# Weight stage of a fused cross-attention, self-attention and expert kernel: scales loaded once and spread by selection matmuls, smaller parts, biases as rows

## The reference

```python
x = x + xattn(layernorm(x), ctx, Wq, w_kc_q, w_kc_kv, W_qr, W_kr, Wo)     # 16 heads, 257 context rows
x = x + attn(layernorm(x), ...)                                           # below
x = x + ffn(layernorm(x), router, gate_up, down)                          # top 8 of 64 experts

def _mxfp4_matmul(x, codes, scales, block_size=32):
    w = codes * jnp.repeat(scales, block_size, axis=0)
    return x @ w
q = _mxfp4_matmul(x, wq_codes, wq_scales) + bq      # codes (256, 2048), scales (8, 2048); k and v likewise
...
return _mxfp4_matmul(out, wo_codes, wo_scales) + bo # codes (2048, 256), scales (64, 256)
```

## Time and profile before

| | us |
|---|---|
| median of three runs | 846.65 |
| span of the profiled execution | 876.3 |
| TensorE matmul busy | 664.1 (76%) |
| VectorE busy | 420.8 (48%) |
| ScalarE busy | 305.1 (35%) |
| GpSimd busy | 291.6 (33%) |
| DMA moved | 92.66 MB |

### The profile page before, as it was taken

The page is one execution under the profiler, slowest core; times in us unless marked ns, Lnnn a source line. Parts: engine busy times, 40 slices in busy tenths (PEclk is TensorE's granted clock), DMA queues, the critical chain, the costliest instruction groups (busy, mean ns, idle before and its releaser), DMA issues.

```text
span 876.3 us, 17897 instructions
## 1 busy us (share of the span) xinstructions
PE 664.1 (76%) x6210; PEld 536.8 (61%) x6210; DVE 420.8 (48%) x1090; ACT 305.1 (35%) x811; POOL 291.6 (33%) x279
## 2 busy tenths in 40 slices
PE   7856777889999997997997997998714765556550
PEld 5745557777867875875875875867513654445440
DVE  1414663454765774774774764756441222222232
ACT  1122553235453362362362363350302333333210
POOL 4003584212114224124124122021224455555562
PEclk8855657799999998998998998999966999999985
DMA  8946994791002002002001001000004989998956
GB/s 244 253 84 154 251 221 120 247 344 27 1 2 79 0 8 70 0 15 63 0 15 63 0 22 38 3 30 30 24 26 120 227 190 200 198 196 198 203 95 168
DMA packets 100680, 92.66 MB, mean 106 GB/s; under 512 B 32366, under 2 KB 94576, under 8 KB 100640
## 3 DMA queue, kind: packets, MB, share of 16 engines
q1 hardware_dynamic: 70992, 60.87, 26.8%
q0 software_dynamic: 12288, 17.95, 10.0%
q10 hardware_dynamic: 17360, 13.30, 5.1%
HBM read 60.22 MB, written 32.83 MB: 106 GB/s over the span
## 4 chain that ended last, share of the span: by engine, by line
PE 42%; DMA 21%; DVE 14%; issue 10%; ACT 5%; another core or an unknown queue 3%; ACTq 2%; SPq 1%; POOL 1%; DVEq 0%; POOLq 0%; PEldq 0%
DMA expert_sums<-Wh,etok 18%; PE bank L1135 5%; PE bank L1137 5%; PE bank L1136 5%; PE bank L1169 4%; PE bank L1201 4%; PE bank L1190 3%; PE bank L1154 3%; PE bank L1238 3%; PE bank L1183 2%; PE bank L1112 1%; ACTq L564 1%; PE bank L1124 1%; PE bank L1182 1%
## 5 line engine op out<-in xcount | busy, mean ns | idle before, releaser
L530 POOL DMA_INDIRECT expert_sums<-Wh,etok x64 | 98.8, 1544 | 96.9 <-DVE Wh L1037 83.0
L1338 PE MATMUL bank<-ring,Wh 96*128 96x256 f32 x128 | 45.0, 434 | 66.1 <-DVE Wh L1025 64.5
L606 ACT ACTIVATE pr<-bank,nmax 128x257 f32<-128x257 f32 x128 | 61.2, 478 | 95.9 <-DVE nmax L830 94.7
L1135 PE MATMUL bank<-space,Wh 128*128 128x128 f16 x512 | 89.4, 221 | 4.9 <-DVE X L928 3.2
L473 POOL DMA_INDIRECT expert_rows<-h,slot x64 | 62.7, 980 | 87.2 <-DVE slot L921 66.6
L1137 PE MATMUL bank<-space,Wl 128*128 128x128 f16 x512 | 89.3, 220 | 0.0
L1136 PE MATMUL bank<-space,Wh 128*128 128x128 f16 x512 | 89.3, 220 | 0.0
L1201 PE MATMUL bank<-Cr,pT 128*128 128x64 f32 x512 | 78.9, 281 | 6.2 <-DVE On L840 5.3
L1201 PEld LDWEIGHTS bank<-Cr,pT 128*128 128x128 f32 x512 | 75.0, 211 | 8.2 <-DVE On L840 5.2
L456 POOL TENSOR_TENSOR Cr<-C,Ct 128x192 f32<-128x192 f32 x64 | 38.4, 625 | 115.9 <-PE bank L1201 114.6
L830 DVE TENSOR_REDUCE nmax<-bank 128x1 f32<-128x257 f32 x128 | 53.4, 419 | 48.6 <-PE bank L1183 43.8
(11 more groups left out here) (173 smaller groups left out, 1518.6 us busy)
## 6 DMA issues: line engine op xcount, KB each, us to landing
ring<-L_ffn_gate_up_proj_dram SPq DMA_DIRECT2D x64, 192.0 KB
expert_rows<-h ACTq DMA_DIRECT2D x8, 1284.0 KB, 13.8
Wh<-expert_rows SPq DMA_DIRECT2D x64, 160.5 KB
ring<-L_ffn_down_proj_dram SPq DMA_DIRECT2D x64, 96.0 KB
C<-ctx_dram SPq DMA_DIRECT2D x24, 128.0 KB, 4.0
expert_sums<-h ACTq DMA_DIRECT2D x2, 1152.0 KB, 14.0
space<-L_xattn_Wo_dram SPq DMA_DIRECT2D x8, 256.0 KB, 5.0
space<-L_xattn_Wq_dram SPq DMA_DIRECT2D x4, 512.0 KB, 8.3
```

The source lines that it names most:

```text
L530: e.indirect_dma_start(Y[n % NY][:, :], bass.IndirectOffsetOnAxis(ap=etok[:, n % 4:n % 4 + 1], axis=0), ye[:, n % 4], None, bounds_check=Y ...
L606: e.activation(pr[:, s, :], bank[r % 2][:, 0:NL], ACT.Exp, bias=nmax[:, s:s + 1], accum_out=rsum[:, s:s + 1]).then_inc(expd, 1)
L1135: e.matmul(dst, ah, bh, start=first and n == 0, stop=False)
L1338: e.matmul(bank[4 + n % 2][:, 0:D], hh[:, n % 2], dn[:, n], start=True, stop=True).then_inc(e_dn, 1)
```

## The change

Parts keep 128 x 1024 elements but have no room for scales: a buffer is half as long, and nine buffers in `space` serve parts 7 to 15, once each; parts 0 to 2 have buffers in `ring` and `diag`, used again by parts 3 to 6. All scales are loaded once, by four loads of 64 KB, each to four partitions (32w to 32w+3). A matrix `pick` of zeros and ones, four rows for each weight, is built by VectorE from the identity. For each part TensorE multiplies it with the scale rows, two f32 matmuls of 512 columns, into two PSUM banks (1 and 6 in the fold, 6 and 7 in tile 0), and VectorE multiplies the codes with these. The fold now takes 1, 2, 2 and 2 parts in groups 0 to 3, and tile 0 nine, in rows 0 to 12. The biases bq, bk and bv are loaded as 48 rows of 128 at the very start and transposed by TensorE together with the router weights. The product of bv and Wo moves from between the tiles into steps 0 to 3 of tile 1, in the place of the output projection that tile 1 doesn't have. SP's order of loads changes: the scales and part 0 stand ahead of the context and group 1, parts 1 and 2 ahead of group 2, part 3 (which waits for part 0) ahead of the rest of group 2, parts 4 to 6 among and behind group 3.

```diff
-FOLD_PARTS = (0, 0, 2, 3)
+FOLD_PARTS = (1, 2, 2, 2)
-TILE_PARTS = dict(zip((0, 2, 3, 5, 6, 8, 9, 11, 12, 14, 15), range(PART0[GROUPS], PARTS)))
-NPB = 6
-BUFFER = [u % 3 for u in range(PART0[GROUPS])]
-BUFFER += [(PART0[GROUPS] % 3 + n) % NPB for n in range(PARTS - PART0[GROUPS])]
+TILE_PARTS = dict(zip((0, 2, 3, 5, 6, 8, 9, 11, 12), range(PART0[GROUPS], PARTS)))
+EARLY = 3
+NPB = EARLY + PARTS - PART0[GROUPS]
+BUFFER = [u % EARLY for u in range(PART0[GROUPS])] + list(range(EARLY, NPB))

...
-        parts = [t.rearrange("p (n f) -> p n f", n=2) for t in (
-            ring[:, 0:2048], ring[:, 2048:4096],
-            diag[:, :, :].rearrange("p a b -> p (a b)"), space[:, 0:2048], space[:, 2048:4096], space[:, 4096:6144])]
+        scl = ring[:, 0:4096]
+        flat_diag = diag[:, :, :].rearrange("p a b -> p (a b)")
+        parts = [ring[:, 4096:5120], flat_diag[:, 0:1024], flat_diag[:, 1024:2048]]
+        parts += [space[:, 1024 * n:1024 * n + 1024] for n in range(NPB - EARLY)]

...
-                elif n >= 3:
+                elif n >= EARLY:
                 if w < 3:
-                    e.dma_start(to[:, 0], codes[w][c * P:(c + 1) * P, o:o + 1024]).then_inc(here, 16)
-                    for q in range(4):
-                        e.dma_start(to[32 * q:32 * q + 32, 1],
-                                    scales[w][4 * c + q:4 * c + q + 1, o:o + 1024].to_broadcast([32, 1024])).then_inc(here, 16)
+                    e.dma_start(to, codes[w][c * P:(c + 1) * P, o:o + 1024]).then_inc(here, 16)
                 else:
-                    e.dma_start(to[:, 0].rearrange("p (h d) -> p h d", h=4),
+                    e.dma_start(to.rearrange("p (h d) -> p h d", h=4),
-                    for q in range(4):
-                        e.dma_start(to[32 * q:32 * q + 32, 1].rearrange("p (h d) -> p h d", h=4),
-                                    scales[w].rearrange("(h q) d -> q h d", q=4)[q:q + 1, hs].to_broadcast([32, 4, D])
-                                    ).then_inc(here, 16)
+            def load_scales(w):
+                to = scl[32 * w:32 * w + 4, :]
+                if w < 3:
+                    e.dma_start(to.rearrange("q (c f) -> q c f", c=2), scales[w].rearrange("(c q) f -> q c f", q=4)).then_inc(scales_in, 16)
+                else:
+                    e.dma_start(to.rearrange("q (h d) -> q h d", h=H), scales[w].rearrange("(h q) d -> q h d", q=4)).then_inc(scales_in, 16)
             def load_context(i):

...
             load_fold_first(0)
             load_fold_rest(0)
+            for w in range(4):
+                load_scales(w)
+            load_part(0)
             load_context(0)
             load_fold_first(1)
             load_fold_rest(1)
+            load_part(1)
+            load_part(2)
             load_fold_first(2)
-            load_part(0)
+            load_part(3)
             load_fold_rest(2)
             load_fold_first(3)
-            load_part(1)
+            load_part(4)
             load_fold_rest(3)
-            load_part(2)
-            for u in range(3, 6):
-                load_part(u)
+            load_part(5)
+            load_part(6)
             e.wait_ge(roped, 2 * BT)
             load_context(1)
-            for u in range(6, PARTS):
+            for u in range(PART0[GROUPS], PARTS):
                 load_part(u)

...
         def _(e):
+            for n, bias in enumerate((bq, bk, bv)):
+                e.dma_start(brows[H * n:H * n + H, :], bias.rearrange("(h p) -> h p", p=P)).then_inc(bias_in, 16)
+            e.dma_start(obias[:, :], bo.unsqueeze(0).to_broadcast([P, D])).then_inc(obias_in, 16)
             def part_high(u):
-                e.copy(part_of(Wh, u), parts[BUFFER[u]][:, 0]).then_inc(w_high, 1)
+                e.copy(part_of(Wh, u), parts[BUFFER[u]]).then_inc(w_high, 1)
             for g in range(GROUPS):

...
                 for u in range(PART0[g], PART0[g + 1]):
-                if g == 1:
-                    with nc.allow_non_contiguous_dma(reason="biases of 2048 elements"):
-                        for n, bias in enumerate((bq, bk)):
-                            e.dma_start(bqk[:, n, :], bias.rearrange("(h p) -> p h", p=P)).then_inc(bias_in, 16)
-                        e.dma_start(bvT[:, :], bv.rearrange("(h p) -> p h", p=P)).then_inc(bias_in, 16)
-                    e.dma_start(obias[:, :], bo.unsqueeze(0).to_broadcast([P, D])).then_inc(bias_in, 16)
             def blank(n):

...
         def _(e):
+            e.wait_ge(consts, 1)
+            for w in range(4):
+                q = slice(32 * w, 32 * w + 4)
+                e.tensor_copy(pick[q, :].rearrange("p (q n) -> p q n", q=4),
+                              ident[q, q].unsqueeze(2).to_broadcast([4, 4, 32])).then_inc(pick_ready, 1)
+            e.tensor_copy(bqk[:, :, :], bank[7][:, P:P + 2 * H].rearrange("p (n h) -> p n h", n=2)).then_inc(rwT_ready, 1)
+            e.tensor_copy(bvT[:, :], bank[7][:, P + 2 * H:P + 3 * H]).then_inc(rwT_ready, 1)

...
-            def part_mul(u):
-                e.wait_ge(w_in[BUFFER[u]], 80 * BUFFER[:u + 1].count(BUFFER[u]))
-                e.scalar_tensor_tensor(parts[BUFFER[u]][:, 0], parts[BUFFER[u]][:, 0], WS, parts[BUFFER[u]][:, 1], ALU.mult, ALU.mult).then_inc(w_mul, 1)
+            def part_mul(u, lo, hi):
+                here = parts[BUFFER[u]]
+                e.wait_ge(w_in[BUFFER[u]], 16 * BUFFER[:u + 1].count(BUFFER[u]))
+                e.wait_ge(w_scaled, u + 1)
+                e.scalar_tensor_tensor(here[:, 0:512], here[:, 0:512], WS, lo[:, :], ALU.mult, ALU.mult)
+                e.scalar_tensor_tensor(here[:, 512:1024], here[:, 512:1024], WS, hi[:, :], ALU.mult, ALU.mult).then_inc(w_mul, 1)
             def rope_copies(g):

...
-                if len(left) > 2:
-                    part_mul(left.pop(0))
+                if len(left) > 1:
+                    part_mul(left.pop(0), bank[1], bank[6])
-                if len(left) > 1:
-                    part_mul(left.pop(0))
+                part_mul(left.pop(0), bank[1], bank[6])
-                for u in left:
-                    part_mul(u)
+                assert not left

...
+            def obias_out():
+                bk_, need = spos("wo", -1)
+                e.wait_ge(sf[bk_], need)
+                e.wait_ge(obias_in, 16)
+                e.scalar_tensor_tensor(obias[:, :], SBANK[bk_][:, 0:D], 1.0 / WS, obias[:, :], ALU.mult, ALU.add).then_inc(sd[bk_], 1)
+                e.wait_ge(sd[bk_], need + FREE)
             def self_out_norm(j):

...
-            ins.then_inc(rw_t, 1)
-            e.wait_ge(rwT_ready, 1)
+            e.wait_ge(bias_in, 48)
+            e.transpose(bank[7][:, P:P + 3 * H], brows, ident[0:3 * H, 0:3 * H]).then_inc(rw_t, 1)
+            e.wait_ge(rwT_ready, 3)
+            def spread_scales(u, lo, hi):
+                if u:
+                    e.wait_ge(w_mul, u)
+                else:
+                    e.wait_ge(pick_ready, 4)
+                    e.wait_ge(scales_in, 64)
+                q = slice(32 * (u // 4), 32 * (u // 4) + 4)
+                o = 1024 * (u % 4)
+                e.matmul(lo[:, :], pick[q, :], scl[q, o:o + 512], start=True, stop=True)
+                e.matmul(hi[:, :], pick[q, :], scl[q, o + 512:o + 1024], start=True, stop=True).then_inc(w_scaled, 1)
             def rope_transposes(g):

...
+                    e.wait_ge(w_mul, PART0[g])

...
+                left = list(range(PART0[g], PART0[g + 1]))
+                if len(left) > 1:
+                    spread_scales(left.pop(0), bank[1], bank[6])

...
                 ins.then_inc(f_n, 1)
+                spread_scales(left.pop(0), bank[1], bank[6])
+                assert not left

...
                     ins.then_inc(sf[bk_], 1)
+            def obias_sum(name):
+                bk_, need = spos("wo", -1)
+                dst = SBANK[bk_]
+                if name == "wo0":
+                    e.wait_ge(sd[bk_], need - 1 + FREE)
+                    e.wait_ge(w_done, PARTS)
+                    e.wait_ge(bv_split, 2)
+                a = 4 * int(name[2])
+                ins = split(dst[:, 0:D], [(bvh[:, h:h + 1].to_broadcast([P, P]), bvl[:, h:h + 1].to_broadcast([P, P]),
+                                           Wh[:, 6 + h // 8, (h % 8) * D:(h % 8 + 1) * D],
+                                           Wl[:, 6 + h // 8, (h % 8) * D:(h % 8 + 1) * D]) for h in range(a, a + 4)],
+                            first=a == 0, last=a == 12)
+                if name == "wo3":
+                    ins.then_inc(sf[bk_], 1)
             def skip(name, j):

...
+                        if isinstance(i, int) and i == 0 and r in TILE_PARTS:
+                            spread_scales(TILE_PARTS[r], *SBANK)

...
             tile(0, None, None)
-            e.wait_ge(w_done, PARTS)
-            e.wait_ge(bv_split, 2)
-            ins = split(bank[7][:, 0:D], [(bvh[:, h:h + 1].to_broadcast([P, P]), bvl[:, h:h + 1].to_broadcast([P, P]),
```

(31 more changed lines are left out.)

## The result

The changed kernel took 901.02 us (median of 4 runs, 892.07 to 902.16) beside 846.74 us for the kernel before (median of 4, 844.25 to 850.82): ratio 1.0603, 95% interval 1.0540 to 1.0666. It is slower by 6.0%, and the forecast of 832.0 us with its range of 815 to 855 missed it. What came true is rival R3, selections at low clock, and it cost more than the 884 us given for its worst form.

What follows compares the result with a forecast made beforehand. Before tile 2, it blamed TensorE's idle hole, low clock and tile 0's scale-row waits and TensorE work. Gains of 8.0 (fold), 1.5 (queries), 0.3 (tile 0) and 4.8 (bias product), 14.6 together, gave 832.0 us, range 815 to 855.

Steps and rivals of the forecast that it cites:

- R3: Rival: clock stays at 0.50 although selections run; 858 us, or 884 with the fold at low clock too; chance 0.14.
- (e): Fold: selection matmuls on TensorE's path, 1.8 us a part, the first 3.6 at low clock; seven parts add 14.4 us.
- (b): Fold: without the hole the clock stays up; groups 2 and 3 save 4.3 us each, group 3's transposes about 0.9.
- (g): Fold, group 0: dense L1118 and first selection raise the clock earlier; L1124 and the next transposes save 1.9 us.
- (d): Fold: scale loads and part 0 ahead of group 1's weights add 5.0 us, with a range of 3 to 10.
- (a): Fold, group 1: bias loads leave ScalarE's queue, removing 12.4 us of idle TensorE; their replacement costs nothing.
- (c): End of fold: no part multiply on VectorE between the last M copy and the first normalised tile; 2.6 us saved.
- (f): Fold: VectorE's multiply in two halves, one operand in PSUM, 1.3 us against 1.2, covered by matmuls; costs 0.
- Tile 0 at full clock: Score rows of tile 0: full clock for rows with parts, 3.05 us each; 40.0 us against 36.0, 4.0 lost.
- Tail and bias product: After tile 0's rows: tail gains 4.3 us; bias product leaving the seam between tiles for tile 1 gains 4.8.
- R2: Rival: SP held by part 3's load until part 0 is subtracted, group 3's weights late; 841 us; chance 0.16, shared.
- R1: Rival: cheap selection, 1.0 us a part; 821 us; chance 0.17.

Runs made afterwards that it cites:

- e1_no_select: The changed kernel without its selection matmuls, VectorE multiplying the codes with themselves, scale loads kept: 869.55 us, ratio 1.0021 to the kernel before.
- e3_bias_only: The kernel before with only the biases loaded as rows at the start and transposed with the router weights: 867.95 us, ratio 0.9982.
- e5_scales_later: The changed kernel with scale loads and part 0 moved behind group 1's first loads: 920.78 us, ratio 1.0521 to the kernel before.
- e10_warm: e4b_bias_product plus two useless 128-row bf16 matmuls behind each score row of tile 0: 849.30 us, ratio 1.0025 to the kernel before.
- e4b_bias_product: The kernel before with bias rows and the product of bv and Wo moved into tile 1, timed again in another group: 844.16 us, ratio 0.9967.
- e2_rows128: The changed kernel with selections over 128 stationary rows instead of 4, the added rows zeros: 879.53 us, ratio 1.0153 to the kernel before.
- e4_bias_product: The kernel before with bias rows and the product of bv and Wo moved into tile 1, first timing: 868.30 us, ratio 0.9952.

## Why the prediction was wrong, step by step

The time is 69.0 us off (901.0, 832.0). Up to the first score of tile 1 the sum said 143.3 (157.9 less 14.6), and 204.3 was measured: 61.0 us of it. The other 8 are not placed; the sum stood on a first profile of before whose 157.9 was 5.6 above the second's. By stage: fold to the last M copy 73.4 forecast, 108.7 measured (+35.3); from there to the first score 11.3 and 14.2 (+2.9); rows of tile 0 40.0 and 63.2 (+23.2); row 15 to the first score of tile 1 18.6 and 18.2 (-0.4).

**The step that failed: (e) with its clock.** The sum took "full clock for part rows" because "wide f32 matmuls raised it" and "the selections are of the wide kind". The number of moving columns was the wrong likeness. L1169 fills 128 rows of the array, the selections four. That, and the score rows at 0.50 while fully busy, the same text filed as arguments for R3, with 0.14. Over 128 rows the same instructions run at 0.92. At the low clock the seven parts of the fold took 25.7 instead of 14.4 us. The 1.8 for a part at full clock was right: 1.82 with 128 rows. In tile 0 the price for the low clock was right: 63.4 in R3, 63.2 measured.

**(b) and (g), clock gained back in the fold: not there.** Groups 1 to 3 took 3.67 or 3.68 for each of L1147 and L1161. That is the 4.3 and 4.3 of (b) never gained, 4.2 lost in group 1, which had had full clock before, and 0.9 and 1.9 of the transposes and of (g): 15.6. e1_no_select and e3_bias_only show that the selections are not needed for it: group 1 lost its clock there as well. What lets the clock fall there stays open; it is not the hole alone, since these kernels have none. The Trainium skill (TensorE: Matmul & The Clock Gate, the HAM clock gate) says that a busy stretch frees the clock and an idle one returns it to half. By that rule the filled hole was bound to help; the trace disagrees here, with 15.00 of 15.00 us busy at 0.51 in group 1 and 30.00 of 30.00 at 0.50 in tile 0.

**(d), late loads: a delay was foreseen, its size and its place were not.** 8.3 us later (14.59 to 22.93) against 5.0 taken and 12 as the far end. The sum priced bytes and landings. What the trace shows is SP's queue: the issue of group 1's first two loads, behind the scales, part 0 and the context, lasts 8.52 us, where it took 1.64 before (9.10 to 10.74); the load that TensorE waits for is issued only then and lands 2.4 us later.

```profile
11.90 8.52 SPq L304 DMA_DIRECT2D space<-L_xattn_W_qr_dram  x2
20.47 0.61 SPq L305 DMA_DIRECT2D space<-L_xattn_W_kr_dram  x1
```

Part 0, issued at 7.68 behind the scales, took 13.0 us to land. The long issue goes with the scale loads: put later (e5_scales_later), they leave group 1's issue at 1.64 and make that of group 2's first two loads 5.79, where it took 1.71 before. The Trainium skill (DMA: Bandwidth & Descriptors, on why a DMA increments its semaphore by 16) has such loads on 4 of 16 engines; the estimate worked out from it, 6.2, was nearer to 8.3. No run counted the engines: from 12 to 18 us the rate was low, 80 to 146 GB/s against 271 in the fold before, but the mean busy share of the 16 engines stood at 1.02 to 1.20, which does not show idle ones.

**(a): the hole went, and its price was given back.** 12.4 us of idle time are not in the trace. Not foreseen: the Wo load, and with it the first fold transposes, came at 10.6 instead of 9.1, for which I had allowed 1 us of room; e3_bias_only, which has the new bias rows and no scale loads, shows the same (10.65). It is no loss of its own in the changed kernel, since TensorE then stands for group 1's weights anyway. With 11.3 of (e), 15.6 of the clock and 3.3 of (d), 30.2 of the fold's 35.3 are placed. The other 5.1 are transposes and G matmuls that took longer than before, 5.8 (1.0 in group 1's first transposes, 0.7, 1.7 and 0.8 in the three rounds of fold transposes, 1.3 in group 3's L1135, 0.3 in group 0), less 0.7 by which the wait for VectorE ahead of group 3 (0.85) came out shorter than taken (1.6).

**(c), 2.6 us behind the last M copy: 0.85 measured.** The part multiply is gone from VectorE there, but the two small instructions that split the value bias and the first normalised tile run beside GpSimd's work (2.12 us from 107.60, 0.98 from 109.68, 0.99 from 110.62) and grew:

```profile
108.70 0.69 DVE L804 COPY M<-bank 128x512 f32<-128x512 f32 x1 [2.25 <-PE bank L1161]
109.31 0.45 DVE L1020 CAST bvh<-bvT 128x16 f16<-128x16 f32 x1
109.78 0.91 DVE L1022 TENSOR_TENSOR bvl<-bvT,bvh 128x16 f16<-128x16 f32 x1
110.62 1.15 DVE L958 TENSOR_SCALAR h<-X,mv,rs 128x256 f32<-128x256 f32 x1
```

Before, the part took 2.69 and the other three 0.16, 0.17 and 0.41. TensorE's wait for the chain fell from 4.10 to 3.25. That is 1.75 of the 2.9 by which this stretch was late; the rest is the 1.5 that L1154 was to gain, of which 0.3 came (5.89 before, 5.59 after).

**(f), multiply in two halves at no cost: right.** L782 and L783 take 0.67 to 0.69 each, in all 16 parts.

**Tile 0 at full clock: nearly right.** With 128 rows the rows took 42.2 and 42.4 us at clocks of 0.92 and 0.90; the sum said 40.0. But that is 6 to 8 us more than before (36.0, 33.9), not 4.0, and no cure for anything: e1_no_select has no waits for parts and its rows take 37.2.

**Tail and bias product: right.** 9.1 forecast in both together, 9.5 measured (27.7 before, 18.2 after), or 7.6 by the second pair of profiles (25.8, 18.2). The product runs in tile 1 between score rows from 204.75 on, at full clock, and the last blanking load's issue ends 32.8 us after the first score; I had said some 32.

**R2** did not come: SP did stand 8.6 us until GpSimd had subtracted part 0, but no fold matmul waits for the loads of group 3. **R1** is excluded by 3.71 us a part.

## What to carry to other kernels

Work that is moved onto TensorE to spare DMA must be priced at the clock that it leaves behind, and here that clock went by how many rows of the array the matmuls fill (0.51 and 0.50 in tile 0 with 4 and 32, 0.92 with 128): a selection over four rows was neither cheaper than one over 128 nor did it lift the clock. Before a wait is cured, put a price on the stage without it, by a kernel that leaves it out: here the hole and the wait for scale rows were plainly to be seen in the trace, and the kernels without them were 0.2% faster and 0.2% slower, both within what the runs can tell from nothing. If anything paid, a little (0.9952 and 0.9967), it was the plainest edit, taking 48 matmuls out of a seam where all engines waited for them. And a load that is slow to issue delays all that stands behind it in its queue: look at the issue times, not only at the bytes.

## What the runs showed of the hardware

- TensorE's clock: 30.00 of 30.00 us busy at 0.50 with about half of the time in four-row f32 matmuls; 0.51 and 0.50 over a tile's rows with 4 and 32 rows, 0.92 and 0.90 with 128, zeros in 124 of them. Two bf16 matmuls of 128 rows a score row raised it from 0.50 to 0.83 (e10_warm beside e4b_bias_product). In the fold an f32 selection over 128 rows lifted it from half to full (e2_rows128, 42.77 to 46.08); the same over four rows did not.
- VectorE's 128x512 f32 multiply with both tensors in SBUF takes 0.68 us alone and up to 2.61 beside GpSimd's subtraction (e1_no_select). With one operand in PSUM all 32 of the changed kernel took 0.67 to 0.69.
- Four loads of 64 KB to four partitions each, with part 0 and the context behind them, went with an issue of the next two loads that held SP for 8.52 us instead of 1.64, with 80 to 146 GB/s moved from 12 to 18 us, and group 1 began 8.3 us later.
- One kernel's fold can run a group at 2.00 or 3.67 us a line from one execution and chip to another: group 2 of the kernel with bias rows and moved product took 2.00 for L1130 in one profile (e4_bias_product) and 3.68 in the other (e4b_bias_product). Which, and why, stays open, and with it some 5 us at the first score of tile 1 (141.1, 145.9).
